# Self-attention on one Trainium2 core: the values' high and low part in one product, and one VectorE step moved

## The chip, the cores and the metric

The kernel runs on one core of a Trainium2 chip. The metric is the device time of one launch in microseconds, median of several runs. The core's engines work side by side, each on its own list of instructions, and meet at semaphores: TensorE (PE in the profile, PEld its weight loads), VectorE (DVE), ScalarE (ACT), GpSimd (POOL) and SyncE (SP), which issues DMAs.

## What is computed

A decoder layer on x of shape (2, 2048, 512), float32: self-attention with 8 heads of 64, cross-attention over 128 context rows, and a two-expert feed-forward block. Only the self-attention is touched:

```python
q, k, v = proj(w_q), proj(w_k), proj(w_v)          # (b, 8, 2048, 64)
qn = _rmsnorm(q, q_gamma) * dh ** (-0.5)
kn = _rmsnorm(k, k_gamma)
sim = jnp.einsum('bhid,bhjd->bhij', qn, kn)
attn = jax.nn.softmax(sim, axis=-1)
out = jnp.einsum('bhij,bhjd->bhid', attn, v)
```

## The kernel before

To keep float32 accuracy with float16 products, a number is held as a high part (rounded to float16) and a low part (what the rounding left). For each batch `b` the attention runs over 32 units: 8 heads times 4 blocks of 512 query rows (`CT`), a block being four row tiles (`TPC`) of 128. A unit runs over the 2048 keys in 8 pairs `p` of two key blocks of 128. Scores stand transposed, keys in partitions, so the weights can go straight into the product with the values.

Per unit and pair the engines do this:

- ScalarE (lines 824 to 836): the exponential of a 128x1024 score tile twice, to float16 (`probs_h`, L828) and to float32 (`probs`, L836). `probs` has two buffers, so L836 of pair p waits until the subtraction of pair p-2 has read its buffer.
- GpSimd (L589 to L597): `probs_l` = `probs` - `probs_h` for every pair but pair 4 (`DVE_PAIR`). `probs_l` also has two buffers: the subtraction of pair p waits (`lo_done`) until TensorE has used the low rows of pair p-2. So pair 5 follows pair 3 on GpSimd and waits for TensorE's low rows of pair 3.
- VectorE: the same subtraction for pair 4 (`probs_low`, L923); 16 row maxima of 128x512 for the unit two further on (`reduce_max`, L909, index `k`), and once per unit their negated maximum (L915); once per unit `output` for the unit before (L935, L937): a reciprocal of the denominators, and one product that scales the four row tiles and writes them to `ko`.
- TensorE (`unit`, L713 on): for each p, in this order: `scores` of pair p+1 (four products of 512 columns, L681 and L682); the maximum product 2p (L666); `values_high` of pair p-1 (L695, L697); the maximum product 2p+1; `values_low` of pair p-2 (L710). "Iteration p" below is this list. The maximum products alternate between two PSUM banks, so product k waits (`mx_free`) until VectorE has reduced k-2. `scores` of pair p+1 waits until L836 of pair p-1 is done.

The values' table `v_hl` has `VW` = 130 columns for a head and key block: 64 of the high part, two columns (the first of which holds ones and yields the denominators), 64 of the low part. `values_high` multiplies each row tile's float16 weights by the first 65 columns (L695) and, in a second product on the same PSUM columns, by the 64 low columns (L697): 16 products for a pair. `values_low` multiplies the low rows by the first 65 columns: 8 products for a pair.

On VectorE the place of `output` and `probs_low` between the maxima is fixed by `unit`: `output` stands behind maximum k = 4, `probs_low` behind maximum 2 * (DVE_PAIR + 1) = 10. Maximum 10 is the first maximum product of TensorE's iteration 5, maximum 9 the second of iteration 4.

Units 2 to 29 run in a loop of two units a turn. Units 30 and 31 have no maxima (there is no later unit), and VectorE splits weights into parts there (L946, L176).

Of the kernel before, what the change touches and what calls it, by code (L numbers as in the profile page):

```python
# [10 lines left out]
ALU = mybir.AluOpType  # L11
# [3 lines left out]
P = 128  # L15
# [13 lines left out]
def decoder_layer(nc, x, ctx_in, ln_g, ln_b, q_gamma, k_gamma, w_q, w_k, w_v, w_o, b_o,  # L29
# [9 lines left out]
    DH = q_gamma.shape[0]  # L39
    H = D // DH  # L40
    TPC = 4
    CT = TPC * P
# [8 lines left out]
    VW = DH + 2 + DH  # L51
    DVE_PAIR = 4
# [32 lines left out]
    with ExitStack() as top:  # L85
        def sem(name):
            return top.enter_context(nc.semaphore(name))
# [7 lines left out]
        pairs = [top.enter_context(nc.psum_tensor(f"bank{i}", [P, 1024], F32)) for i in range(4)]  # L95
# [138 lines left out]
        nm_ready = sem("nm_ready")  # L234
        m_ready = sem("m_ready")
        o_rec = sem("o_rec")
        o_free = sem("o_free")

        c_ctx = sem("c_ctx")
# [193 lines left out]
        for b in range(B):  # L433
# [8 lines left out]
            with ExitStack() as attn:  # L442
# [3 lines left out]
                v_hl = sb(attn, "v_hl", [P, KB * H * VW], F16)  # L446
# [7 lines left out]
                with ExitStack() as ph:  # L454
# [12 lines left out]
                    sq = sb(ph, "sq", [P, D], F32)  # L467
# [16 lines left out]
                    OB = banks[6:8]  # L484
# [8 lines left out]
                    U0 = b * UNITS  # L493
                    LA = 2
                    MAXED = UNITS - LA
                    AHEAD = 6
                    vf = v_hl
                    next_h = {"o": share4[0], "xq": share4[1]}
                    next_l = {"o": share4[2], "xq": share4[3]}
# [57 lines left out]
                    @block.gpsimd  # L557
                    def _(pool):
                        def ones():
                            pool.wait_ge(a_xn, T0 + 3)  # L560
                            pool.nop(nofuse=True)
                            pool.memset(k_h1[DH:DH + 1, :, :].rearrange("p h n -> p (h n)").bitcast(F32), TWO_ONES)\
                                .then_inc(a_ones, 1)
                            pool.wait_ge(a_ones, 2 * b + 1)
                            pool.nop(nofuse=True)

                        def step(t, s, before, next1, next2):
                            if next2:
                                row_scale(pool, b, t + 2, s)
                                row_normalise(pool, b, t + 2, s)  # L570
                                row_affine(pool, b, t + 2, s)
                            if not before:
                                ones()

                        for t in range(KB):
                            step(t, t % 2, t > 0, t + 1 < KB, t + 2 < KB)

                        pool.wait_ge(a_ssq, (T0 + KB) * 2 + 1)
                        pool.nop(nofuse=True)  # L580
                        pool.memset(nm0[:, :, :], 0.0).then_inc(e_zero, 1)

                        pool.wait_ge(a_v_done, T0 + KB)
                        pool.nop(nofuse=True)
                        pool.memset(v_hl[:, :].rearrange("p (k e) -> p k e", e=VW)[:, :, DH:DH + 1], 1.0)\
                            .then_inc(a_ones, 1)
                        pool.wait_ge(a_ones, 2 * b + 2)
                        pool.nop(nofuse=True)
                        with pool.Fori(0, UNITS) as u:  # L589
                            G = (U0 + u) * PAIRS  # L590
                            for p in range(PAIRS):
                                if p == DVE_PAIR:
                                    continue
                                pool.wait_ge(p_ready, G + p + 1)

                                pool.wait_ge(lo_done, G + p + 1)
                                pool.tensor_tensor(probs_l[:, p % 2, :], probs[:, p % 2, :], probs_h[:, p % 4, :],  # L597
                                                   ALU.subtract).then_inc(pl_pool, 1)

                    @block.tensor  # L600
                    def _(pe):
# [83 lines left out]
                        def values_high(u, p, ob):  # L685
                            pe.wait_ge(ph_ready, (U0 + u) * PAIRS + p + 1)
                            if p == 0:

                                pe.wait_ge(o_free, U0 + u + 1)
                            for half in range(2):  # L690
                                v0 = (2 * p + half) * (H * VW) + u // CH * VW
                                for t in range(TPC):
                                    rows = probs_h[:, p % 4, half * CT + t * P:half * CT + t * P + P]
                                    o0 = t * (DH + 1)
                                    pe.matmul(ob[:, o0:o0 + DH + 1], rows, vf[:, bass.ds(v0, DH + 1)],  # L695
                                              start=(p == 0 and half == 0 and t == 0), stop=False, skip_group_check=True)
                                    pe.matmul(ob[:, o0:o0 + DH], rows, vf[:, bass.ds(v0 + DH + 2, DH)],  # L697
                                              start=False, stop=False, skip_group_check=True)

                        def values_low(u, p, ob):  # L700

                            if p == DVE_PAIR:
                                pe.wait_ge(pl_dve, U0 + u + 1)
                            else:
                                pe.wait_ge(pl_pool, low_count(u, p))
                            for half in range(2):
                                v0 = (2 * p + half) * (H * VW) + u // CH * VW
                                for t in range(TPC):
                                    o0 = t * (DH + 1)
                                    mm = pe.matmul(ob[:, o0:o0 + DH + 1],  # L710
                                                   probs_l[:, p % 2, half * CT + t * P:half * CT + t * P + P],
                                                   vf[:, bass.ds(v0, DH + 1)], start=False,
                                                   stop=(p == PAIRS - 1 and half == 1), skip_group_check=True)  # L713
                            mm.then_inc(lo_done, 1)

                        def unit(u, s, first=False, maxed=True, last=False):
                            for p in range(PAIRS):
# [4 lines left out]
                                for half in range(2):  # L722
                                    if first:

                                        for k in range(2):
                                            if p * 4 + half * 2 + k >= AHEAD:
                                                unit_max(1 + p // 4, p % 4 * 4 + half * 2 + k)
# [20 lines left out]
                        for a in range(TPC):  # L748
                            mm = pe.matmul(OB[0][0:DH + 1, a * P:(a + 1) * P], nm0[:, a, :], eye16[:, :],
                                           start=True, stop=True)  # L750
                        mm.then_inc(e_row, 1)
                        for k in range(2, AHEAD):
                            unit_max(1, k)
# [85 lines left out]
                    def _(dve):  # L839
# [86 lines left out]
                        def o_out(u):  # L926
                            first = u // (2 * CH) * (CH * TPC * P) + u % CH * (TPC * P) + u // CH % 2 * DH
                            return of[:, bass.ds(first, TPC * P)].rearrange("p (t d) -> p t d", d=P)[:, :, 0:DH]

                        def output(u, s):  # L930

                            o4 = OB[s][:, 0:TPC * (DH + 1)].rearrange("p (t e) -> p t e", e=DH + 1)
                            r4 = rden[:, :].rearrange("p (t a) -> p t a", a=1)
                            dve.wait_ge(lo_done, (U0 + u + 1) * PAIRS + 2)
                            dve.reciprocal(r4, o4[:, :, DH:DH + 1]).then_inc(o_rec, 1)  # L935
                            dve.wait_ge(o_rec, U0 + u + 1)
                            dve.tensor_tensor(o_out(u), o4[:, :, 0:DH], r4.broadcast_to([P, TPC, DH]), ALU.mult)\  # L937
                                .then_inc(o_free, 1)

                        def split_both(pieces):  # L940

# [8 lines left out]
                        def unit(u, s, first=False, maxed=True):  # L950
                            if first:
                                for k in range(AHEAD, 16):
                                    reduce_max(1, k, 1)
                                negate_max(1, 1)
                            for k in range(16):
                                if maxed:
                                    reduce_max(u + LA, k, s)
                                if k == 4 and not first:
                                    output(u - 1, 1 - s)
                                if k == (6 if first else 2 * (DVE_PAIR + 1)):  # L960
                                    probs_low(u)
                            if maxed:
                                negate_max(u + LA, s)
# [1637 lines left out]
```

## Time and profile before

| what | before |
|---|---|
| device time, median of 3 runs (lowest, highest) | 2322.66 us (2322.13, 2323.05) |
| profiled execution: own time, span | 2315.09 us, 2313.3 us |
| TensorE busy | 2178.3 us, 94% |
| ScalarE busy | 1612.0 us, 70% |
| VectorE busy | 1552.2 us, 67% |
| GpSimd busy | 1542.5 us, 67% |
| mean granted TensorE clock | 0.992 |

The attention units of the first batch lie at about 190 to 751 us of the span and those of the second at about 1339 to 1900 us. A timeline row gives start, duration, engine, line, operation, tiles and count, and in brackets how long the engine had been idle and what released it. Starts are those of the engine: an instruction may start a little before the end of the one in front of it (they overlap in the pipeline), and a TensorE product's end is modelled. A duration holds time in which an instruction has started and is held up, so a long duration of a kind that otherwise has one fixed duration is a wait that no idle time shows.

### The profile page before, as it was taken

The page shows a single profiled execution, that of the slowest core. Times are in us where ns is not written, and L with a number is a line of the kernel's source. Part 1 is how long each engine was busy: PE and PEld are TensorE (multiplying, and loading weights), DVE is VectorE, ACT ScalarE, POOL GpSimd, SP SyncE. Part 2 cuts the span into 40 slices and gives each one's busy share as a digit, 9 for nine tenths or more (in the row PEclk, how much of TensorE's full clock was granted, in tenths as well). Part 3 has the DMA queues.
Part 4 walks back from the last instruction along what each step waited for, and adds up shares of the span by engine and source line. Part 5 has one row for each costly group of instructions (what it writes and reads, how often), then busy time and mean ns, then how long its engine had stood idle before and what let it go on. Part 6 is the DMA issues. An engine that isn't in the chain of part 4 may idle for free. (4 is left out here: it accounts for less than half of the span.)

```text
span 2313.3 us, 62611 instructions
## 1 busy us (share of the span) xinstructions
PE 2178.3 (94%) x22392; PEld 1254.6 (54%) x22392; DVE 1552.2 (67%) x2573; ACT 1612.0 (70%) x1831; POOL 1542.5 (67%) x1008
## 2 busy tenths in 40 slices
PE   6988999999997989899989899999999978998999
PEld 3544666666665455444445456666666644554444
DVE  5897777777776666753368977777777767667532
ACT  3556999999998556731145579999999975566210
POOL 5644988989988577721246368998989976867210
PEclk9999999999999999999999999999999999999999
DMA  4220000000001301103112100000000022021000
GB/s 105 56 49 3 4 7 9 9 9 9 9 0 28 100 6 39 46 12 81 46 51 56 42 1 10 0 9 9 9 9 9 9 61 64 2 47 38 19 23 33
DMA packets 102348, 65.23 MB, mean 28 GB/s; under 512 B 75346, under 2 KB 75346, under 8 KB 102226
## 3 DMA queue, kind: packets, MB, share of 16 engines
q1 hardware_dynamic: 102226, 63.57, 12.5%
q8 instruction: 81, 1.33, 0.2%
q14 instruction: 41, 0.34, 0.1%
HBM read 46.69 MB, written 8.39 MB: 24 GB/s over the span
## 5 line engine op out<-in xcount | busy, mean ns | idle before, releaser
L597 POOL TENSOR_TENSOR qkn<-wide 128x1024 f16<-128x1024 f32 x448 | 986.7, 2234 | 136.5 <-PE bank L710 120.7
L909 DVE TENSOR_REDUCE sq<-bank 128x1 f32<-128x512 f32 x1024 | 679.8, 688 | 246.8 <-PE bank L666 244.1
L836 ACT ACTIVATE wide<-bank,shift 128x1024 f32<-128x1024 f32 x512 | 571.0, 1115 | 37.3 <-DVE qkn L923 30.7
L828 ACT ACTIVATE wide<-bank,shift 128x1024 f16<-128x1024 f32 x512 | 568.1, 1110 | 9.9 <-PE bank L682 9.9
L681 PE MATMUL bank<-q_hh,ko 128*128 (+1 forms) x1024 | 388.9, 380 | 18.5 <-ACT wide L836 13.6
L666 PE MATMUL bank<-ko,q_hh 128*128 (+1 forms) x1024 | 387.7, 380 | 10.7 <-DVE sq L909 7.1
L682 PE MATMUL bank<-q_lm,k_h 65*128 (+1 forms) x1024 | 389.0, 380 | 0.0
L695 PEld LDWEIGHTS bank<-v_hl,wide 128*128 128x128 f16 x4096 | 287.6, 98 | 63.4 <-issue 5.7
L695 PE MATMUL bank<-v_hl,wide 128*128 (+1 forms) x4096 | 320.0, 192 | 0.1
L697 PE MATMUL bank<-v_hl,wide 128*128 (+1 forms) x4096 | 318.1, 193 | 0.0
L697 PEld LDWEIGHTS bank<-v_hl,wide 128*128 128x128 f16 x4096 | 267.5, 96 | 58.7
L710 PEld LDWEIGHTS bank<-v_hl,qkn 128*128 128x128 f16 x4096 | 187.6, 97 | 63.9 <-POOL qkn L597 10.7
L710 PE MATMUL bank<-v_hl,qkn 128*128 (+1 forms) x4096 | 208.0, 193 | 9.5 <-POOL qkn L597 9.4
L1263 POOL TENSOR_TENSOR wide<-wide 128x1024 f16<-128x1024 f32 x64 | 139.7, 2198 | 86.7 <-ACT wide L1940 86.5
L666 PEld LDWEIGHTS bank<-ko,q_hh 128*128 (+1 forms) x1024 | 99.5, 97 | 105.4 <-DVE sq L909 27.0
L2167 ACT ACTIVATE q<-bank,b1c 128x512 f32<-128x512 f32 x48 | 33.0, 688 | 172.5 <-PE bank L189 172.5
L681 PEld LDWEIGHTS bank<-q_hh,ko 128*128 (+1 forms) x1024 | 99.3, 97 | 83.5 <-ACT wide L836 18.1
L682 PEld LDWEIGHTS bank<-q_lm,k_h 65*128 (+1 forms) x1024 | 99.3, 97 | 63.2
L331 POOL TENSOR_SCALAR rs_a<-mv_a 128x1 f32<-128x1 f32 x32 | 7.0, 217 | 185.1 <-DVE mv_a L325 184.5
L2209 DVE TENSOR_REDUCE nmt<-bank 128x4 f16<-128x512 f32 x128 | 83.6, 692 | 49.9 <-PE bank L1510 49.6
L775 ACT ACTIVATE sq<-bank 128x512 f32<-128x512 f32 x64 | 38.2, 597 | 103.0 <-PE bank L189 92.6
L1407 POOL TENSOR_TENSOR q_lm<-q_lm,ko 128x512 f32<-128x512 f32 x24 | 30.7, 1311 | 109.4 <-DVE ko L2307 73.2
(228 smaller groups left out, 4213.2 us busy)
## 6 DMA issues: line engine op xcount, KB each, us to landing
wide<-in_x SPq DMA_DIRECT2D x32, 256.0 KB, 2.7
q_lm<-in_x SPq DMA_DIRECT2D x32, 256.0 KB, 3.2
ko<-in_L_ffn_W SPq DMA_DIRECT2D x32, 256.0 KB, 4.1
q_hh<-q_hh SPq DMA_DIRECT2D x32, 128.0 KB, 2.6
ko<-k_h SPq DMA_DIRECT2D x32, 128.0 KB, 2.8
out<-bo_b SPq DMA_DIRECT2D x16, 256.0 KB, 2.0
out<-xbo_b SPq DMA_DIRECT2D x16, 256.0 KB, 2.0
q_lm<-sq SPq DMA_DIRECT2D x248, 0.2 KB, 4.9
```

What stands on the lines that cost most here:

```text
L597: pool.tensor_tensor(probs_l[:, p % 2, :], probs[:, p % 2, :], probs_h[:, p % 4, :], ALU.subtract).then_inc(pl_pool, 1)
L666: pe.matmul(MB[k % 2], qf[:, bass.ds(r * CT + k // 4 * P, P)], k1[:, bass.ds(r // CH * N + k % 4 * CT, CT)], start=True, stop=True)\
L681: pe.matmul(bank, k1[:, kcols], qf[:, qcols], start=True, stop=False)
L682: mm = pe.matmul(bank, k2[0:DH + 1, kcols], lf[0:DH + 1, qcols], start=False, stop=True)
L695: pe.matmul(ob[:, o0:o0 + DH + 1], rows, vf[:, bass.ds(v0, DH + 1)], start=(p == 0 and half == 0 and t == 0), stop=False, skip_group_check ...
L697: pe.matmul(ob[:, o0:o0 + DH], rows, vf[:, bass.ds(v0 + DH + 2, DH)], start=False, stop=False, skip_group_check=True)
L710: mm = pe.matmul(ob[:, o0:o0 + DH + 1], probs_l[:, p % 2, half * CT + t * P:half * CT + t * P + P], vf[:, bass.ds(v0, DH + 1)], start=Fals ...
L828: act.activation(probs_h[:, p % 4, :], SB[p % 2][:, :], ACT.Exp, bias=shift[:, 0:1]).then_inc(ph_ready, 1)
L836: act.activation(probs[:, p % 2, :], SB[p % 2][:, :], ACT.Exp, bias=shift[:, 0:1]).then_inc(p_ready, 1)
L909: dve.tensor_reduce(pm[:, s, k:k + 1], MB[k % 2], AX_X, ALU.max).then_inc(mx_free, 1)
L1263: pool.tensor_tensor(pxl[:, k % 2, :], px[:, k % 2, :], pxh[:, k % 2, :], ALU.subtract)\
L2209: dve.tensor_reduce(nmt[:, j, d::32], tile_bank("sm", c, i).rearrange("p (a k) -> p a k", k=CTX), AX_X, ALU.max, negate=True).then_inc(d_n ...
```

## The change

`values_high` gives the three row tiles t = 0, 1, 2 (`WIDE` = 3) one product with all 130 columns each: columns 0 to 64 collect the high part and the denominators as before, columns 66 to 129 the low part by itself (column 65 is a second column of ones and isn't used). The fourth row tile keeps its two products, since four times 130 columns don't fit a PSUM bank of 512. `values_low` writes where the high part stands. So the sum of high and low part, which PSUM made for all tiles, is now made by `output` for three tiles: it scales the high parts (four tiles), scales the low parts (three tiles) into `o_low`, 192 columns of the small SBUF tile `sq`, waits for both, and adds `o_low` to what it wrote to `ko`. Both operands of that sum lie in SBUF. The signal `o_free`, on which TensorE may overwrite the bank, stands on the second product. Apart from that, `probs_low` stands behind maximum 2 * DVE_PAIR + 1 = 9 instead of 10, and GpSimd writes two columns of ones where it wrote one.

```diff
+                    WIDE = TPC - 1
+                    o_low = sq[:, 300:300 + WIDE * DH].rearrange("p (t e) -> p t e", e=DH)
...
-                        pool.memset(v_hl[:, :].rearrange("p (k e) -> p k e", e=VW)[:, :, DH:DH + 1], 1.0)\
+                        pool.memset(v_hl[:, :].rearrange("p (k e) -> p k e", e=VW)[:, :, DH:DH + 2], 1.0)\
                             .then_inc(a_ones, 1)
...
-                                    o0 = t * (DH + 1)
-                                    pe.matmul(ob[:, o0:o0 + DH + 1], rows, vf[:, bass.ds(v0, DH + 1)],
+                                    o0 = t * VW
+                                    wide = VW if t < WIDE else DH + 1
+                                    pe.matmul(ob[:, o0:o0 + wide], rows, vf[:, bass.ds(v0, wide)],
                                               start=(p == 0 and half == 0 and t == 0), stop=False, skip_group_check=True)
-                                    pe.matmul(ob[:, o0:o0 + DH], rows, vf[:, bass.ds(v0 + DH + 2, DH)],
-                                              start=False, stop=False, skip_group_check=True)
+                                    if t >= WIDE:
+                                        pe.matmul(ob[:, o0:o0 + DH], rows, vf[:, bass.ds(v0 + DH + 2, DH)],
+                                                  start=False, stop=False, skip_group_check=True)
...
-                                    o0 = t * (DH + 1)
+                                    o0 = t * VW
                                     mm = pe.matmul(ob[:, o0:o0 + DH + 1],
...
                         def output(u, s):
 
-                            o4 = OB[s][:, 0:TPC * (DH + 1)].rearrange("p (t e) -> p t e", e=DH + 1)
+                            skip = s * (TPC * VW - CT)
+                            four = pairs[3][:, s * CT - skip:s * CT - skip + TPC * VW].rearrange("p (t e) -> p t e", e=VW)
+                            high, den = four[:, :, skip:skip + DH], four[:, :, skip + DH:skip + DH + 1]
+                            low = OB[s][:, 0:WIDE * VW].rearrange("p (t e) -> p t e", e=VW)[:, :, DH + 2:]
                             r4 = rden[:, :].rearrange("p (t a) -> p t a", a=1)
+                            o_u = o_out(u)
                             dve.wait_ge(lo_done, (U0 + u + 1) * PAIRS + 2)
-                            dve.reciprocal(r4, o4[:, :, DH:DH + 1]).then_inc(o_rec, 1)
+                            dve.reciprocal(r4, den).then_inc(o_rec, 1)
                             dve.wait_ge(o_rec, U0 + u + 1)
-                            dve.tensor_tensor(o_out(u), o4[:, :, 0:DH], r4.broadcast_to([P, TPC, DH]), ALU.mult)\
+                            dve.tensor_tensor(o_u, high, r4.broadcast_to([P, TPC, DH]), ALU.mult).then_inc(o_sum, 1)
+                            dve.tensor_tensor(o_low, low, r4[:, 0:WIDE, :].broadcast_to([P, WIDE, DH]), ALU.mult)\
                                 .then_inc(o_free, 1)
+                            dve.wait_ge(o_sum, U0 + u + 1)
+                            dve.wait_ge(o_free, U0 + u + 3)
+                            dve.tensor_tensor(o_u[:, 0:WIDE, :], o_u[:, 0:WIDE, :], o_low, ALU.add)
...
-                                if k == (6 if first else 2 * (DVE_PAIR + 1)):
+                                if k == (6 if first else 2 * DVE_PAIR + 1):
                                     probs_low(u)
```

## Rows read from the trace of the kernel before

**Rows 1.** The page: the span, and each engine's busy time.

```profile
span 2313.3 us, 62611 instructions
PE 2178.3 (94%) x22392; PEld 1254.6 (54%) x22392; DVE 1552.2 (67%) x2573; ACT 1612.0 (70%) x1831; POOL 1542.5 (67%) x1008
```

**Rows 2.** Windows view, units of batch 0: busy PE, PEld, DVE, ACT, POOL; clock; DMA.

```profile
260.00:700.00 440.00, 437.26 (x6180) 283.05 (x6177) 316.82 (x515) 428.19 (x413) 393.06 (x181) 1.00 0.08 8
```

**Rows 3.** Timeline, GpSimd: three units, each from pair 5 on.

```profile
415.89 15.31 POOL L597 TENSOR_TENSOR qkn<-wide 128x1024 f16<-128x1024 f32 x7 [1.92 <-PE bank L710]
432.81 15.31 POOL L597 TENSOR_TENSOR qkn<-wide 128x1024 f16<-128x1024 f32 x7 [1.62 <-PE bank L710]
450.05 6.95 POOL L597 TENSOR_TENSOR qkn<-wide 128x1024 f16<-128x1024 f32 x3 [1.92 <-PE bank L710]
```

**Rows 4.** Timeline, GpSimd, single instructions: pair 2 and pair 5.

```profile
426.98 2.13 POOL L597 TENSOR_TENSOR qkn<-wide 128x1024 f16<-128x1024 f32 x1
...
432.81 2.77 POOL L597 TENSOR_TENSOR qkn<-wide 128x1024 f16<-128x1024 f32 x1 [1.62 <-PE bank L710]
```

**Rows 5.** Timeline, VectorE, the same unit: maximum 4, output, maxima 5 to 10, probs_low.

```profile
425.49 0.69 DVE L909 TENSOR_REDUCE sq<-bank 128x1 f32<-128x512 f32 x1 [0.64 <-PE bank L666]
426.10 0.17 DVE L935 RECIPROCAL sq<-bank 128x4 f32<-128x4 f32 x1
426.91 0.42 DVE L937 TENSOR_TENSOR ko<-bank,sq 128x256 f32 x1 [0.64 <-DVE sq L935]
427.25 1.88 DVE L909 TENSOR_REDUCE sq<-bank 128x1 f32<-128x512 f32 x3
...
431.77 0.69 DVE L909 TENSOR_REDUCE sq<-bank 128x1 f32<-128x512 f32 x1 [0.64 <-PE bank L666]
432.38 1.22 DVE L923 TENSOR_TENSOR qkn<-wide 128x1024 f16<-128x1024 f32 x1
```

**Rows 6.** Timeline, TensorE products, the same unit, end of iteration 3 to iteration 5.

```profile
427.10 0.38 PE L666 MATMUL bank<-ko,q_hh 128*128 x1
...
427.99 0.39 PE L666 MATMUL bank<-ko,q_hh 128*128 x1
428.21 0.41 PE L710 MATMUL bank<-v_hl,qkn 128*128 x8
428.46 0.38 PE L681 MATMUL bank<-q_hh,ko 128*128 x1
...
429.33 0.38 PE L666 MATMUL bank<-ko,q_hh 128*128 x1
...
430.02 0.38 PE L666 MATMUL bank<-ko,q_hh 128*128 x1
430.24 0.41 PE L710 MATMUL bank<-v_hl,qkn 128*128 x8
430.48 0.38 PE L681 MATMUL bank<-q_hh,ko 128*128 x1
...
432.26 0.41 PE L710 MATMUL bank<-v_hl,qkn 128*128 x8
```

**Rows 7.** Timeline, ScalarE: pair 6's float32 exponential in two units.

```profile
433.63 1.12 ACT L836 ACTIVATE wide<-bank,shift 128x1024 f32<-128x1024 f32 x1 [0.28 <-DVE qkn L923]
...
450.86 1.12 ACT L836 ACTIVATE wide<-bank,shift 128x1024 f32<-128x1024 f32 x1 [0.58 <-DVE qkn L923]
```

**Rows 8.** Timelines of GpSimd and VectorE in units 30 and 31, without maxima.

```profile
719.72 2.12 POOL L597 TENSOR_TENSOR qkn<-wide 128x1024 f16<-128x1024 f32 x1
...
720.95 1.99 DVE L923 TENSOR_TENSOR qkn<-wide 128x1024 f16<-128x1024 f32 x1 [5.87 <-ACT wide L836]
...
723.57 3.03 DVE L176 SCALAR_TENSOR_TENSOR share<-q_lm,share 128x1024 f16<-128x1024 f32 x1
...
725.48 3.12 POOL L597 TENSOR_TENSOR qkn<-wide 128x1024 f16<-128x1024 f32 x1
```

**Rows 9.** Line 923 by itself: least, median and greatest duration in ns.

```profile
L923 DVE TENSOR_TENSOR qkn<-wide x64: 1215/1215/1993, 208.2 to 1887.6; 128x1024 f16<-128x1024 f32 x64
```

More of the change, by code:

```diff
@@ L236, in decoder_layer @@
         o_rec = sem("o_rec")
+        o_sum = sem("o_sum")
         o_free = sem("o_free")
```

## The prediction

> **What bounds the kernel now.** I read the page first: TensorE is busy 94% of the span [rows 1]. The change touches only the attention units, so the next view is the busy time of a stretch of them: TensorE 437.3 of 440 us, ScalarE 428.2, GpSimd 393.1, VectorE 316.8 [rows 2]. Three engines are near their limit and the busy shares don't say which one sets the pace; the timeline does. GpSimd's seven subtractions of a unit run end to end, then it idles 1.62 or 1.92 us for TensorE's low rows of pair 3 [rows 3]. Its pair 5 starts at 415.89, 432.81 and 450.05: two units in 34.16 us, **17.08 us a unit**, 16.92 and 17.24 in turn (the longer one holds the turn of the loop).
>
> Four things are to be seen inside a unit.
> - TensorE's iteration takes 428.46 to 430.48, 2.02 us, without a wait: scores 0.87, maximum and 16 high products 0.69, maximum 0.22, eight low products 0.24 [rows 6]. Eight make 16.2 us; the 0.9 us left are waits. One is at maximum 7: its PSUM bank comes free when VectorE, late from `output`, ends maximum 5 at 427.25 + 0.69 = 427.94; the product starts at 427.99, 0.89 us behind product 6 at 427.10 instead of 0.69 [rows 5, 6].
> - GpSimd's subtraction takes 2.13 us alone and 2.77 for pair 5 [rows 4]; without that excess the pitch is (15.31 - 2.77) / 6 = 2.09 us [rows 3, 4].
> - The excess of pair 5 is `probs_low` on VectorE: it runs 432.38 to 433.60, GpSimd starts at 432.81, and its end is 0.64 us late [rows 4, 5]. Units 30 and 31 show the opposite order. There L923 starts at 720.95, while a subtraction that began at 719.72 is under way, and takes 1.99 us instead of its median of 1.22; 722.94 - 1.22 = 721.72 is 2.00 us behind GpSimd's start. L176, which also reads two SBUF tiles, takes 3.03 us, and the subtraction behind it 3.12 [rows 8, 9]. So a VectorE instruction with two SBUF inputs and GpSimd's subtraction exclude each other for a whole instruction, and whoever comes second waits. L937, with one input in PSUM, keeps its 0.42 us at 426.91 and pair 2 its 2.13 at 426.98 [rows 4, 5]: it isn't concerned.
> - ScalarE waits 0.28 and 0.58 us a unit for L923 [rows 7].
>
> The Trainium skill, page "SBUF — State Buffer", section "Who interferes with whom", says the same of the kind of instruction: the port pair that VectorE and GpSimd share is an exclusive lock for a whole instruction, and a `tensor_tensor` with both inputs in SBUF takes it against GpSimd's reads. By that rule the new sum is caught, and it is the rule that speaks against this change.
>
> **The change, part by part.** *Wide products.* Per pair six products with their weight loads go; the columns multiplied rise by one per tile, 129 to 130. Four score products take 0.87 us, 0.2175 each; 512 columns at the full clock of 2.4 GHz (granted clock 1.00, rows 2) are 0.2133. Eight products of 65 columns take 0.24, 0.030 each, of which 0.0271 are columns [rows 6]. So a product costs 0.003 to 0.004 us beyond its columns, and six fewer save about **0.02 us a pair**, 0.16 us a unit. No row shows a 130-column product. The bounds are nothing (if the extra only moves) and 6 x 0.03 = 0.18 us a pair (if a wide product cost what a narrow one does, which the 512-column rows exclude); I take 0.02, since the two sizes agree on the extra. The skill's page "TensorE: Matmul & The Clock Gate", section "Back-to-back issue gap", gives some 81 ns for a load and product pair of 128 columns in a stream; by it 16 pairs would take over 1 us and a saving of several tenths a pair could follow. Here 16 narrow products take 0.69 - 0.22 = 0.47 us with their loads.
>
> *`probs_low` one maximum sooner.* Behind maximum 9 its place on VectorE comes one TensorE half iteration, 0.69 to 1.3 us, earlier. Its input, pair 4's float32 exponential, is then ready, and GpSimd is in its idle time before pair 5. Taken alone this ends ScalarE's 0.28 and 0.58 us [rows 7] and the 0.64 us excess [rows 4].
>
> *The longer `output`.* From rows 5 and 9, VectorE's 256 columns take 0.42 us and 1024 take 1.22: 1.04 ns a column and 0.16 fixed, so 192 columns take 0.36. Instructions follow 0.08 before the end of the one in front (426.91 to 427.25). The second product adds 0.28. The sum waits for that product, so it loses the overlap and a semaphore's 0.1, and adds 0.46. Without more that is 0.75 us. The address registers fill the 0.64 us before L937; I count them once, as `o_u` is one expression. If the sum computed them anew, its request would come 0.5 us later, which changes nothing as long as it stays inside the same subtraction.
>
> But the sum reads two SBUF tiles while GpSimd runs end to end. In the rows it would ask at 427.25 + 0.36 + 0.1 = 427.71, 0.73 us into pair 2's subtraction [rows 4, 5]. It has to wait until 426.98 + 2.00 = 428.98, and maximum 5 starts at 429.26 instead of 427.25, two microseconds late. Queued behind the sum are all further maxima; TensorE waits for maximum 5 with product 7, and behind product 7 stand the low rows of pair 1, for which GpSimd's pair 3 waits, and the scores that ScalarE needs. Nothing covers this: product 7 waits 0.2 us for VectorE already [rows 6], so the cover is used up.
>
> *The new unit.* The stall feeds itself. A closed chain, from the start of GpSimd's pair 2 to that of the next unit:
> - until GpSimd lets the sum in: 2.00 [rows 8]
> - sum until the next maximum starts: 0.28
> - maximum 5, and the signal to TensorE: 0.69 + 0.06 [rows 5, 6]
> - product 7 and eight low products: 0.46 [rows 6]
> - iteration 4: 2.02 - 0.02 = 2.00
> - iteration 5 up to the low rows of pair 3: 432.26 - 430.48 - 0.02 = 1.76
> - until pair 5 starts on GpSimd: 432.81 - 432.26 = 0.55 [rows 3, 6]
> - pairs 5, 6, 7, 0, 1: 5 x 2.09 = 10.45
>
> The sum is **18.25 us**. L923 lies inside GpSimd's idle time in it, so pair 5 has no excess. The loop's turn cost 0.32 before; with slack on TensorE between iterations 6 and 3 I leave 0.1 of it, every second unit: **18.30** on average, 1.22 more than 17.08.
>
> Maxima and `output` meet in 29 units a batch (1 to 29), so 58 x 1.22 = 70.8 us. In units 30 and 31 no maxima queue behind the sum. The last `output` of a batch is exposed: 2 x 0.75 = 1.5. The second column of ones is one small GpSimd write a batch, hidden by VectorE's and TensorE's opening maxima. Total +72.3: on the profiled execution 2315.09 + 72.3 = 2387.4 us, on the median, which stands 7.6 us above it, 2322.66 + 72.3 = **2395.0 us**.
>
> **The rivals.** *A, the change gives what its two parts free.* If `output`'s extra time were hidden, the unit would fall to GpSimd's and TensorE's common chain: pair 3 with the idle time behind it, 2.13 + 1.62 = 3.75, and six pitches of 2.09, 16.3 [rows 3, 4]; this sum gives the 16.92 of before once the 0.64 are added. With the loop's turn that is some 16.5. 58 x -0.6 = -35: 2288 us. For it: two real waits go. Against it: the 0.75 us on VectorE, with no cover at product 7. Chance 0.08.
>
> *B, no exclusion for so small a sum, or GpSimd is not under way when it asks.* Then product 7 comes 0.75 us later (428.74), which TensorE's chain carries, and gives back 0.64 from pair 5 and 0.1 from the products: 17.1 to 17.3 us a unit, 2322 to 2335, middle 2328. Against it: every case in the rows where the two met was serial. Chance 0.10.
>
> *C, the sum asks late in the subtraction.* The stall is fixed by where the request falls: 0.73 us into pair 2 now, and about 1 us once TensorE lags. If other waits moved it to the last half microsecond, part of the stall would be time that TensorE had lost anyway; 17.7 us a unit, 2358 us. Chance 0.08.
>
> *D, a second collision.* If `probs_low`, now earlier, asks while pair 3 is still under way (it did in rows 8), it waits too and holds maxima 10 and 11: up to 0.7 us a unit more, 19.0, 2435. Against it: pair 3 starts behind the stall, and iteration 4 with its maximum 9 does too, so pair 3 ends some tenths before L923 is due. Chance 0.04.
>
> **How the numbers follow.** Forecast 0.70, A 0.08, B 0.10, C 0.08, D 0.04. The forecast's own range is 18.1 to 18.45 us a unit, 2383 to 2404. The range reaches past C and into D's smaller sizes, and leaves out A, B and half of D, 20%: 2345 to 2415. A measurement can tell 0.2%, 4.6 us. Faster: A and a fifth of B, 0.10. Within 0.2%: half of B, 0.05. Slower: the rest of B, C, D and the forecast, 0.85.
>
> **What would show it.** Right: GpSimd's row of seven is broken between pairs 2 and 3; the new sum has a duration of 1.0 to 1.5 us instead of 0.36; product 7 starts 1 us or more behind the low rows' place; pair 5 lasts 2.13; the wait of L836 for L923 is gone; starts of pair 5 are 18.3 apart. Wrong: the sum at 0.36 us beside a running subtraction (B), or VectorE idle for TensorE behind `output` (A).

## The result and the profile after

The changed kernel takes **2422.23 us** (median of 4 runs, 2416.89 to 2426.61) against 2322.39 us for the kernel before: a ratio of 1.043 (95% interval 1.0404 to 1.0456), 99.8 us slower. The direction was as forecast. The forecast size was 72.3 us, and 2422 lies above the range's end of 2415.

The page of the changed kernel, its head and the lines of part 5 that answer to GpSimd's subtraction, the maximum product and the narrow products:

```profile
span 2415.1 us, 56659 instructions
PE 2178.7 (90%) x19320; PEld 1245.6 (52%) x19320; DVE 1662.4 (69%) x2701; ACT 1615.6 (67%) x1831; POOL 1503.0 (62%) x1008
...
L600 POOL TENSOR_TENSOR qkn<-wide 128x1024 f16<-128x1024 f32 x448 | 951.5, 2152 | 268.4 <-PE bank L715 252.2
...
L669 PE MATMUL bank<-ko,q_hh 128*128 (+1 forms) x1024 | 395.3, 388 | 117.8 <-DVE sq L914 115.4
```

There are 3072 fewer products (22392 before, rows 1). VectorE is busy 110 us longer, though the two new instructions of a unit need 0.71 us, 45 us in 64 units. The rest is time in which the sum had started and was held: its 64 instructions last 87.2 us together, 23 us at 0.36 each. TensorE now stands 115.4 us for VectorE ahead of the maximum products.

The output of one unit on VectorE, as in rows 5 (L946 was L937, L947 and L951 are new):

```profile
482.37 0.69 DVE L914 TENSOR_REDUCE sq<-bank 128x1 f32<-128x512 f32 x1 [0.64 <-PE bank L669]
482.98 0.17 DVE L944 RECIPROCAL sq<-bank 128x4 f32<-128x4 f32 x1
483.79 0.42 DVE L946 TENSOR_TENSOR ko<-bank,sq 128x256 f32 x1 [0.64 <-DVE sq L944]
484.13 0.35 DVE L947 TENSOR_TENSOR sq<-bank,sq 128x192 f32<-128x192 f32 x1
484.58 1.57 DVE L951 TENSOR_TENSOR ko<-ko,sq 128x192 f32 x1
486.08 2.07 DVE L914 TENSOR_REDUCE sq<-bank 128x1 f32<-128x512 f32 x3
```

L951 asks at 484.58 and takes 1.57 us. The line by itself (least, median, greatest in ns), and L928, which was L923:

```profile
L951 DVE TENSOR_TENSOR ko<-ko,sq x64: 358/1314/1997, 222.5 to 1998.8; 128x192 f32 x56, 128x192 f32<-128x192 f32 x8
...
L928 DVE TENSOR_TENSOR qkn<-wide x64: 1215/1215/1992, 208.9 to 1986.6; 128x1024 f16<-128x1024 f32 x64
```

GpSimd in that stretch. First the subtraction that the sum meets, pair 2, and then the row of subtractions, as in rows 3:

```profile
483.81 2.13 POOL L600 TENSOR_TENSOR qkn<-wide 128x1024 f16<-128x1024 f32 x1
```

```profile
455.14 12.56 POOL L600 TENSOR_TENSOR qkn<-wide 128x1024 f16<-128x1024 f32 x6 [1.88 <-PE bank L715]
469.36 2.13 POOL L600 TENSOR_TENSOR qkn<-wide 128x1024 f16<-128x1024 f32 x1 [1.65 <-PE bank L715]
473.37 12.57 POOL L600 TENSOR_TENSOR qkn<-wide 128x1024 f16<-128x1024 f32 x6 [1.88 <-PE bank L715]
488.01 2.12 POOL L600 TENSOR_TENSOR qkn<-wide 128x1024 f16<-128x1024 f32 x1 [2.07 <-PE bank L715]
493.18 12.56 POOL L600 TENSOR_TENSOR qkn<-wide 128x1024 f16<-128x1024 f32 x6 [3.05 <-PE bank L715]
```

The sum asks 484.58 - 483.81 = 0.77 us into pair 2's subtraction, and ends at 486.15 = 483.81 + 2.00 + 0.34: it waits for all of what is left. In the other unit of the loop's turn it asks 1.02 to 1.13 us into pair 2 and lasts 1.21 to 1.31 us (here pair 2 starts at 465.58), so it too is let go 2.00 us behind the start of pair 2:

```profile
466.61 1.31 DVE L951 TENSOR_TENSOR ko<-ko,sq 128x192 f32 x1
```

TensorE's standstill ahead of maximum product 7 alternates with it: 1.98 to 2.03 us in 28 units and 1.67 to 1.83 in 30, those with the later request and the first of each batch. The row of seven is broken in two places: six, then pair 3 alone. Pair 5 starts at 455.14 and at 473.37, **18.23 us** apart; it ends without the 0.64 us excess of rows 4. The next distance is 19.81 us (493.18). Over the 56 distances between units 1 and 29 of both batches the starts of L928 are mostly 18.23 to 18.28 apart, but 21 of them are 18.8 to 19.9.

What happens in a long unit is to be seen on TensorE. The timeline behind one standstill, weight loads left out:

```profile
261.61 0.61 PE L669 MATMUL bank<-ko,q_hh 128*128 x1 [1.98 <-DVE sq L914]
262.01 0.65 PE L715 MATMUL bank<-v_hl,qkn 128*128 x8
262.47 0.62 PE L684 MATMUL bank<-q_hh,ko 128*128 x1
262.87 0.63 PE L685 MATMUL bank<-q_lm,k_h 65*128 x1
263.30 0.63 PE L684 MATMUL bank<-q_hh,ko 128*128 x1
```

and, for comparison, score products of another unit, ahead of its standstill:

```profile
483.08 0.38 PE L684 MATMUL bank<-q_hh,ko 128*128 x1
483.30 0.38 PE L685 MATMUL bank<-q_lm,k_h 65*128 x1
483.52 0.38 PE L684 MATMUL bank<-q_hh,ko 128*128 x1
```

The score products follow each other every 0.43 us in the first and 0.22 in the second. The granted clock says why (windows view, changed kernel; first the 4 us above, then a quiet stretch ahead of it, then the attention stretch of rows 2):

```profile
core 0: us, PE busy (x) PEld busy (x) DVE busy (x) ACT busy (x) POOL busy (x), PEclk, DMA share, GB/s
261.00:265.00 4.00, 3.39 (x21) 1.80 (x22) 2.01 (x4) 1.48 (x2) 2.12 (x1) 0.57 0.00 0
241.00:259.00 18.00, 16.25 (x193) 10.47 (x192) 13.93 (x24) 16.44 (x17) 14.46 (x8) 1.00 0.03 2
260.00:700.00 440.00, 395.22 (x4489) 252.37 (x4490) 330.65 (x516) 391.00 (x375) 342.19 (x164) 0.97 0.07 7
```

### The profile page after: what moved, and what is told of

Read it like the earlier page. It is cut to its first block and busy times, and to the rows that moved or that the text cites. A ratio compares the mean times of both kernels' runs of the same rounds, so it can differ in the third digit from the quotient of the medians.

```text
span 2415.1 us, 56659 instructions
## 1 busy us (share of the span) xinstructions
PE 2178.7 (90%) x19320; PEld 1245.6 (52%) x19320; DVE 1662.4 (69%) x2701; ACT 1615.6 (67%) x1831; POOL 1503.0 (62%) x1008
## 5 line engine op out<-in xcount | busy, mean ns | idle before, releaser
L600 POOL TENSOR_TENSOR qkn<-wide 128x1024 f16<-128x1024 f32 x448 | 951.5, 2152 | 268.4 <-PE bank L715 252.2
L669 PE MATMUL bank<-ko,q_hh 128*128 (+1 forms) x1024 | 395.3, 388 | 117.8 <-DVE sq L914 115.4
L684 PE MATMUL bank<-q_hh,ko 128*128 (+1 forms) x1024 | 397.2, 388 | 14.1 <-ACT wide L841 14.0
L685 PE MATMUL bank<-q_lm,k_h 65*128 (+1 forms) x1024 | 398.3, 389 | 0.0
L699 PEld LDWEIGHTS bank<-v_hl,wide 128*128 128x128 f16 x4096 | 279.0, 98 | 126.6 <-issue 15.4
L699 PE MATMUL bank<-v_hl,wide 128*128 (+2 forms) x4096 | 309.5, 215 | 0.1
L702 PE MATMUL bank<-v_hl,wide 128*128 (+1 forms) x1024 | 200.4, 196 | 0.0
L684 PEld LDWEIGHTS bank<-q_hh,ko 128*128 (+1 forms) x1024 | 101.3, 99 | 77.6 <-ACT wide L841 18.3
L702 PEld LDWEIGHTS bank<-v_hl,wide 128*128 128x128 f16 x1024 | 101.3, 99 | 0.0
```

The source lines that it names most:

```text
L669: pe.matmul(MB[k % 2], qf[:, bass.ds(r * CT + k // 4 * P, P)], k1[:, bass.ds(r // CH * N + k % 4 * CT, CT)], start=True, stop=True)\
L684: pe.matmul(bank, k1[:, kcols], qf[:, qcols], start=True, stop=False)
L685: mm = pe.matmul(bank, k2[0:DH + 1, kcols], lf[0:DH + 1, qcols], start=False, stop=True)
L699: pe.matmul(ob[:, o0:o0 + wide], rows, vf[:, bass.ds(v0, wide)], start=(p == 0 and half == 0 and t == 0), stop=False, skip_group_check=True)
```

## The experiments

Two theories were open after the result. The first: the stall comes from the meeting of the sum and GpSimd's subtraction, and the excess over 18.24 us from the clock. Its rivals: the stall comes from `output` being longer with more waits, and the long units from another order of the engines. The kernels of one group ran on one chip beside the kernel before; its median there is given each time. Unit times are mean distances of L928 (L923) starts over units 1 to 29 of both batches; it is 17.12 us before and 18.79 in the changed kernel by that measure.

**The sum with one SBUF operand.**

The sum reads the unscaled low columns from PSUM in place of what stands in `ko`, so the result is wrong for three row tiles. As it now reads the bank, the signal `o_free` moves onto it.

```diff
     dve.tensor_tensor(o_low, low, r4[:, 0:WIDE, :].broadcast_to([P, WIDE, DH]), ALU.mult)\
-        .then_inc(o_free, 1)
-    dve.wait_ge(o_sum, U0 + u + 1)
-    dve.wait_ge(o_free, U0 + u + 3)
-    dve.tensor_tensor(o_u[:, 0:WIDE, :], o_u[:, 0:WIDE, :], o_low, ALU.add)
+        .then_inc(o_sum, 1)
+    dve.wait_ge(o_sum, 2 * (U0 + u + 1))
+    dve.tensor_tensor(o_u[:, 0:WIDE, :], low, o_low, ALU.add).then_inc(o_free, 1)
```

> The changed kernel, but the sum reads the low columns from PSUM in place of the SBUF tile it has just written: same size, same number of instructions and waits, one SBUF operand instead of two. The result lacks the right low part of three row tiles (unscaled columns are added). Theory (the exclusion between GpSimd and a VectorE instruction with two SBUF operands makes the stall): the sum lasts 0.36 us, product 7 waits under 1 us, unit 17.1 to 17.3, 2325 to 2335, no dips of the clock in the attention units. Rival (the stall comes from the length and the waits of output as such): 2400 or above, as the changed kernel.

Measured: 2318.32 us against 2319.51, ratio 0.999 (0.9981 to 1.0), unit 17.10 us. VectorE's timeline, and then the line of the sum by itself:

```profile
444.92 0.35 DVE L947 TENSOR_TENSOR sq<-bank,sq 128x192 f32<-128x192 f32 x1
445.30 0.36 DVE L950 TENSOR_TENSOR ko<-bank,sq 128x192 f32 x1
445.57 1.87 DVE L914 TENSOR_REDUCE sq<-bank 128x1 f32<-128x512 f32 x3
```

```profile
L950 DVE TENSOR_TENSOR ko<-bank,sq x64: 357/357/358, 223.0 to 1900.3; 128x192 f32 x56, 128x192 f32<-128x192 f32 x8
```

All 64 sums last 357 or 358 ns, though 62 of them start with a subtraction of GpSimd under way, and the loss is gone (2325 to 2335 had been expected, the unit came as expected). Nothing but where one operand lies was changed in this instruction's work, so the stall is the exclusion. What is left of a longer `output` eats what the other two edits give: the kernel is as fast as before.

**The standstill filled with products.** TensorE repeats maximum product 6 five times ahead of its signal.

```diff
+    FILL = 5
...
+    if 2 * p + half == 6:
+        r, k = u + LA, 6
+        pe.wait_ge(mx_free, (U0 + r) * 16 + k + 1)
+        for _ in range(FILL):
+            pe.matmul(MB[k % 2], qf[:, bass.ds(r * CT + k // 4 * P, P)], k1[:, bass.ds(r // CH * N + k % 4 * CT, CT)],
+                      start=True, stop=True)
     unit_max(u + LA, 2 * p + half)
```

> The changed kernel, but TensorE repeats the maximum product 6 five times before it signals it, 1.1 us of work in the place where it otherwise stands still ahead of product 7; what it computes is the same. Theory (the units of 19.8 us among those of 18.24 are those in which TensorE's clock falls to half after its standstill of 1.8 us): the granted clock stays 1.00 through the units, all are 18.2 to 18.35 us, 2390 to 2396, about 27 us less than the changed kernel though TensorE does more. Rival (the long units come from something else, a GpSimd or ScalarE order that flips): the long units stay, 2415 to 2430, or more if the added products count.

Measured: 2385.14 us against 2319.51, ratio 1.0283 (1.0265 to 1.03). All 56 distances between units 1 and 29 are 18.22 to 18.25 us, mean 18.24, and TensorE's waits ahead of product 7 are 0.64 to 0.94 us. The time is 5 us under the 2390 expected. The granted clock of the stretch, and product 7 in one unit:

```profile
260.00:700.00 440.00, 419.67 (x4748) 265.82 (x4745) 339.46 (x532) 401.96 (x386) 353.43 (x170) 1.00 0.07 7
```

```profile
443.60 0.39 PE L670 MATMUL bank<-ko,q_hh 128*128 x1 [0.94 <-DVE sq L922]
```

With 290 products more, doing nothing new, the kernel is 37 us faster than the changed one by the medians, and 34 us if each is taken against the kernel before on its own chip (65.6 us above it instead of 99.8). The long units are the clock's; with the stall alone a unit lasts 18.24 us, whatever TensorE does meanwhile. This kernel was timed on one chip only.

**No sum at all**, and **the sum in GpSimd's idle time**. In the first, the three lines of the sum are left out, so the result lacks the low part of three row tiles:

```diff
-    dve.wait_ge(o_sum, U0 + u + 1)
-    dve.wait_ge(o_free, U0 + u + 3)
-    dve.tensor_tensor(o_u[:, 0:WIDE, :], o_u[:, 0:WIDE, :], o_low, ALU.add)
```

In the second they stand in a function of their own (`output_sum`), called behind maximum 9 and, for a batch's last unit, behind the last `output`:

```diff
     if k == (6 if first else 2 * DVE_PAIR + 1):
+        if not first:
+            output_sum(u - 1)
         probs_low(u)
```

> The changed kernel without the sum: the low part of three row tiles is scaled into the small tile and not added, so it is missing from the result. Theory: everything above 16.7 us a unit in the changed kernel comes from the sum; 16.7 to 16.8 us, 2295 to 2305, like the kernel with the sum in the gap. Rival (second product or the wide products carry a part of the loss): 17.1 us or more, 2320 or above.

> The changed kernel with the whole result, but the sum of two SBUF operands stands right ahead of probs_low behind maximum 9, where GpSimd idles for the low rows of pair 3. Theory (only a meeting with a running subtraction costs; the instruction as such 0.36 us): the sum lasts 0.36 us in nearly all units, the unit falls to 16.7 to 16.8 us, 2295 to 2305, faster than before. Rival (the exclusion holds whether or not GpSimd is executing, or the meeting moves to pair 3): sums of 1 us and more, 2380 or above.

Measured: without the sum 2296.28 us against 2320.28, 0.9892 (0.9876 to 0.9908), unit 16.72; with the sum in the gap 2298.37, 0.9896 (0.9882 to 0.991), unit 16.72 too. The latter's VectorE timeline:

```profile
424.03 1.37 DVE L914 TENSOR_REDUCE sq<-bank 128x1 f32<-128x512 f32 x2 [0.62 <-PE bank L669]
425.31 0.35 DVE L954 TENSOR_TENSOR ko<-ko,sq 128x192 f32 x1
425.58 1.22 DVE L928 TENSOR_TENSOR qkn<-wide 128x1024 f16<-128x1024 f32 x1
```

and GpSimd's, idle from 425.18 to 427.06:

```profile
416.77 8.41 POOL L600 TENSOR_TENSOR qkn<-wide 128x1024 f16<-128x1024 f32 x4
427.06 12.56 POOL L600 TENSOR_TENSOR qkn<-wide 128x1024 f16<-128x1024 f32 x6 [1.87 <-PE bank L715]
```

The same instruction that lasts 1.57 us behind maximum 4 lasts 0.35 here, and costs nothing that can be measured: the unit is the same as without it, and the runs of both kernels overlap.

The unit times of four kernels now split the loss: 16.72 us without the sum, 17.10 with the sum from PSUM, which isn't held, 18.24 with the held sum and the clock kept up, and 18.79 in the changed kernel. So the sum's own time in that place costs 0.38 us a unit, the meeting 1.13 and the clock 0.55; in 58 units some 22, 66 and 32 us. Against them stand the 23 us that the rest of the change gives (16.72 instead of 17.12).

**The parts alone.** `probs_low` behind maximum 9 in the kernel before, run in two groups:

```diff
-    if k == (6 if first else 2 * (DVE_PAIR + 1)):
+    if k == (6 if first else 2 * DVE_PAIR + 1):
```

> The kernel before with the one edit that probs_low stands behind maximum 9 instead of 10. Theory (the two waits it removes are real and close together on the chain that sets the unit): ScalarE's waits of 0.28 and 0.58 us for L923 and the 0.64 us excess of GpSimd's pair 5 go, the unit falls from 17.1 to 16.5 us, 58 units give -30 to -35 us: about 2290. Rival (another chain, say TensorE's eight iterations with its waits for VectorE, sets the unit anyway): 2315 to 2325.

> The kernel before with probs_low behind maximum 9 once more, to stand on one chip beside the fused sum in the gap: 2290 to 2296, unit 16.65 us.

Measured: 2293.59 us, 0.9888 (0.9871 to 0.9904), and 2293.99, 0.9883 (0.9866 to 0.9901); unit 16.65 both times, where 16.5 had been expected of the first. GpSimd:

```profile
428.81 14.85 POOL L597 TENSOR_TENSOR qkn<-wide 128x1024 f16<-128x1024 f32 x7 [1.74 <-PE bank L710]
```

The seven last 14.85 us instead of the 15.31 of rows 3, and pair 5 by itself 2.13 instead of 2.77: its excess is gone. ScalarE's wait for L923 is no longer among its waits. The stretch of rows 2 in this kernel:

```profile
260.00:700.00 440.00, 439.50 (x6357) 284.76 (x6355) 328.55 (x530) 438.42 (x424) 388.58 (x186) 1.00 0.08 9
```

The wide products alone, with `output` as before the change, so that the low part of three row tiles is missing:

```diff
-    dve.tensor_tensor(o_u, high, r4.broadcast_to([P, TPC, DH]), ALU.mult).then_inc(o_sum, 1)
-    dve.tensor_tensor(o_low, low, r4[:, 0:WIDE, :].broadcast_to([P, WIDE, DH]), ALU.mult)\
-        .then_inc(o_free, 1)
-    dve.wait_ge(o_sum, U0 + u + 1)
-    dve.wait_ge(o_free, U0 + u + 3)
-    dve.tensor_tensor(o_u[:, 0:WIDE, :], o_u[:, 0:WIDE, :], o_low, ALU.add)
+    dve.tensor_tensor(o_u, high, r4.broadcast_to([P, TPC, DH]), ALU.mult).then_inc(o_free, 1)
...
-    if k == (6 if first else 2 * DVE_PAIR + 1):
+    if k == (6 if first else 2 * (DVE_PAIR + 1)):
```

> The kernel before with the wide products alone: output is a reciprocal and one product as before, so the low part of three row tiles is left out of the result; probs_low stands behind maximum 10 as before. Theory (six products fewer a pair save their 3 ns each, and TensorE isn't what the unit waits for alone): a product of 130 columns every 0.057 us, unit 17.0 to 17.1 us, 2318 to 2323. Rival (the saving per pair reaches the end in full or is larger, weight loads count): 0.16 us a unit or more, 2313 or below.

Measured: 2316.08 us against 2319.51, 0.9986 (0.9976 to 0.9995), unit 17.05; this lies between what was expected and its rival. The high products of one pair:

```profile
429.71 0.38 PE L669 MATMUL bank<-ko,q_hh 128*128 x1
429.92 0.36 PE L699 MATMUL bank<-v_hl,wide 128*128 x4
430.12 0.19 PE L702 MATMUL bank<-v_hl,wide 128*128 x1
430.15 0.36 PE L699 MATMUL bank<-v_hl,wide 128*128 x4
430.35 0.19 PE L702 MATMUL bank<-v_hl,wide 128*128 x1
430.38 0.38 PE L669 MATMUL bank<-ko,q_hh 128*128 x1
```

From maximum to maximum 0.67 us, where rows 6 have 0.69: 0.02 us a pair, as put into the sum. Of the 10 us that this makes in 512 pairs, 3.4 reach the end.

**`probs_low` behind maximum 10 in the changed kernel**, the edit above undone there.

> The changed kernel with probs_low behind maximum 10 again. Theory: the 0.64 us excess of GpSimd's pair 5 comes back into the same chain as the stall, so the unit's undisturbed pitch rises by 0.6 to 0.8, from 18.24 to 18.9 to 19.05 us, plus the clock's dips: 2445 to 2470. Rival (beside the stall the place of probs_low has no weight, its gain having been another chain's): 2415 to 2430.

Measured: 2464.5 us against 2320.28, 1.0632 (1.0609 to 1.0655). GpSimd's timeline:

```profile
438.01 13.23 POOL L600 TENSOR_TENSOR qkn<-wide 128x1024 f16<-128x1024 f32 x6 [1.89 <-PE bank L715]
...
456.90 4.87 POOL L600 TENSOR_TENSOR qkn<-wide 128x1024 f16<-128x1024 f32 x2 [1.88 <-PE bank L715]
```

Pair 5 to pair 5 is 18.89 us, 0.66 more than 18.23, and the six last 13.23 instead of 12.57. The excess of 0.64 lies in full in the chain of the stall. The kernel is 144.2 us above the kernel before on its chip, the changed one 99.8, so the sooner place is worth 44 us in the changed kernel: 38 in 58 units of 0.66 us, and the rest in more falls of the clock (23 distances of 20.5 us).

**Fused sums.** One instruction for each of three row tiles takes the low columns from PSUM, multiplies by the reciprocal as a scalar and adds what stands in `ko`; nothing is left out. First behind maximum 4 (the edit below), then with the same three instructions in a function of their own, called behind maximum 9 ahead of `probs_low`:

```diff
-    dve.tensor_tensor(o_low, low, r4[:, 0:WIDE, :].broadcast_to([P, WIDE, DH]), ALU.mult)\
-        .then_inc(o_free, 1)
     dve.wait_ge(o_sum, U0 + u + 1)
-    dve.wait_ge(o_free, U0 + u + 3)
-    dve.tensor_tensor(o_u[:, 0:WIDE, :], o_u[:, 0:WIDE, :], o_low, ALU.add)
+    for t in range(WIDE):
+        last = dve.scalar_tensor_tensor(out=o_u[:, t, :], in0=low[:, t, :], scalar=rden[:, t:t + 1],
+                                        in1=o_u[:, t, :], op0=ALU.mult, op1=ALU.add)
+    last.then_inc(o_free, 1)
```

> The changed kernel with the whole result, but second product and sum are one instruction for each of the three row tiles: low columns from PSUM, times the reciprocal as a scalar, plus what stands in ko; one SBUF tile operand. Theory (exclusion makes the loss, the rest of output costs its own time only): three instructions of 0.22 us at a pitch of some 0.15 instead of 0.36 + 0.36 and a wait; nothing above 0.3 us; unit about 17.0 us, 2312 to 2320, no clock dips in the units. Rival (an instruction with one SBUF operand and a pointer to a scalar in SBUF is held up by GpSimd too): durations of 1 us and more, 2380 or above.

> The changed kernel with the whole result: output behind maximum 4 is a reciprocal and one product as before the change; the low parts are added behind maximum 9, ahead of probs_low, by one instruction for each of three row tiles that reads the low columns from PSUM (0.28 us each as measured, some 0.2 apart). Theory (both findings add up: nothing longer behind maximum 4, nothing with two SBUF tiles but probs_low itself, which stands in GpSimd's idle time): unit 16.45 to 16.6 us, 2282 to 2292, the fastest of all. Rival (ScalarE or GpSimd sets 16.65 us, or the three instructions ahead of probs_low bring ScalarE's wait for it back): 2293 to 2300, no better than probs_low one maximum sooner by itself.

Measured: behind maximum 4, 2322.97 us against 2320.28, 1.0009 (1.0 to 1.0019), unit 17.15; behind maximum 9, 2298.11 against 2320.66, 0.9908 (0.9894 to 0.9922), unit 16.72. VectorE behind maximum 4 in the first of them:

```profile
428.83 0.42 DVE L946 TENSOR_TENSOR ko<-bank,sq 128x256 f32 x1 [0.64 <-DVE sq L944]
429.29 0.67 DVE L949 SCALAR_TENSOR_TENSOR ko<-bank,sq,ko 128x64 f32 x3
429.88 1.87 DVE L914 TENSOR_REDUCE sq<-bank 128x1 f32<-128x512 f32 x3
```

An instruction with one SBUF tile and a scalar from SBUF isn't held: behind maximum 4 all 192 of them last 272 to 285 ns, 186 with a subtraction under way. But here my expectation of the time missed on both. From L946 to the next maximum it is 1.05 us, where the sum from PSUM above has 1.00, so three small instructions take as long as product and sum together; and the fused sum in the gap isn't the fastest, its rival stands.

The three kernels with wide products and no sum behind maximum 4 (no sum, sum in the gap, fused sum in the gap; 16.72 us each) are a little slower than `probs_low` alone (16.65), so the 0.02 us a pair doesn't show in them. In the stretch of rows 2 ScalarE is busy 438.4 of 440 us in `probs_low` alone and 436.7 to 437.6 in these three. That ScalarE now sets the unit is argued from this and was not tested.

## Why the prediction was right and where it was wrong

**What bounds the kernel, right.** Three engines in one closed chain, and the two waits that the sooner `probs_low` ends: alone it gives 26 us. Rival A's 35 for both parts together was high; neither the kernel without the sum nor `probs_low` alone comes under 16.65 us, where A put 16.5.

**The exclusion, right, and the step that decided.** It was read from a few instructions in units 30 and 31 [rows 8]. The request came 0.77 us into pair 2 in one unit (0.73 from the rows) and 1.02 to 1.13 in the next ("about 1 us once TensorE lags"), the hold ended 2.00 us behind that pair's start as put, and the sum with one SBUF operand removed the whole loss. The Trainium skill's page "SBUF — State Buffer", section "Who interferes with whom", calls the port pair that VectorE and GpSimd share an exclusive lock; the trace agrees in both directions: 1.57 us for the sum behind a running subtraction, 2.77 for a subtraction behind `probs_low` [rows 4].

**The closed chain, right.** Its sum was 18.25 us; undisturbed units are 18.23 to 18.25, and so are all in the kernel with the filled standstill, to 0.01 us. The terms hold one by one: from pair 2 at 465.58 to maximum 5 2.26 us (2.28 in the sum), to product 7 0.74 (0.75), to iteration 4 0.47 (0.46), iteration 4 2.00, to the low rows of pair 3 1.76, to pair 5 0.56 (0.55), to the next pair 2 10.44 (10.45). The 0.05 left for the loop's turn was wrong: there is none. Rival B's unit without the meeting, 17.1 to 17.3, is what the sum from PSUM shows, 17.10.

**The wide products, right**: 0.02 us a pair, and 0.056 us for 130 columns.

**The step that failed: the sum has no term for TensorE's clock.** I priced a TensorE that stands 1.7 to 2.0 us a unit as if the granted clock stayed at 2.4 GHz; in 19 of the 58 units it fell to 1.2. Between the first and the last L928 of a batch lie 578.6 and 580.6 us, 96.0 more in both than before. In the kernel with the filled standstill these are 564.2 and 564.2, 65.2 more than before. So 65 us are the stall, and **31 us the clock**, 1.6 us for each of the 19 falls. Against the forecast: stall 65.2 instead of 70.8 (17.12 instead of 17.08 before, 18.24 instead of 18.30 after), clock 30.8 instead of nothing, and outside the units 5.8 us instead of 1.5. Some 6 us more out there come without this change too. Outside the stretches from the first to the last subtraction on VectorE the profiled execution of the kernel before has 1250.1 us, the changed kernel 1255.8, and `probs_low` alone, whose code there is that of the kernel before, 1256.1 and 1256.3. The profiled execution of the kernel before had fewer falls of the clock there: 38 us at 1.2 GHz, against 55 to 58 in those three. So the 4 us beyond the forecast's 1.5 are the execution's and not a cost of the change, and whether the 1.5 are real can't be told beside them. With the clock's term the forecast would have been 2395 + 31 = 2426, and the range, moved by as much, would have held 2422.

It could have been foreseen that there might be such a term, though not its size. TensorE's busy share in the units falls from 99% to 90%, and a fall of that size follows from the forecast itself (eight iterations of 2.00 us in 18.3, 87%). The kernel before also has falls beside idle time: its granted clock was 1.00 in the stretch of attention units [rows 2] and 0.992 on the whole, so its falls lay elsewhere, for one at the end of a batch, where TensorE is busy 12.05 of 20 us and the granted clock is 0.74 (windows view, columns as in rows 2):

```profile
740.00:760.00 20.00, 12.05 (x130) 7.35 (x129) 15.56 (x14) 8.71 (x10) 9.82 (x5) 0.74 0.40 119
```

The Trainium skill's page "TensorE: Matmul & The Clock Gate", section "HAM oscillation — how this bites in real kernels", describes such a fall in a loop that waits at every turn; its example waits 3 to 5 us a turn. Here waits of 1.98 to 2.03 us were followed by a fall in 17 of 28 units and waits of 1.67 to 1.83 in 2 of 30, and in the kernel with the filled standstill waits of 0.64 to 0.94 never.

**The faster version.** The change's two ideas with the sum moved by five maxima give 2298.4 us, and `probs_low` one maximum sooner in the kernel before, one number in one line, gives 2293.6 to 2294.0: 26 us faster than before, and 126 faster than the changed kernel (each against the kernel before on its own chip). The last is the one to keep; both are faster than before by about 1%, clear of the intervals.
